# Kept rows turned by VectorE in 32x32 blocks and stored features outermost, in place of transposes on TensorE

## The reference

```python
def _L0_attn_ref(x, w_gate, w_up, w_down):
    s = jax.nn.silu(jnp.einsum('bsh,ih->bsi', x, w_gate))     # I = 2752 features
    k = int(0.5 * I)
    _, idx = jax.lax.top_k(-jnp.abs(s), k)                    # the half smallest in magnitude, per token
    flat = flat.at[rows, idx.reshape(B * S, k)].set(0.0)      # ... become zero
    s = s * jnp.einsum('bsh,ih->bsi', x, w_up)
    return jnp.einsum('bsi,hi->bsh', s, w_down)
```

## Time and profile before

| | |
|---|---|
| median of 3 runs | 1417.43 us (1416.8 to 1418.82) |
| span of the profiled execution | 1417.5 us |
| TensorE matmuls busy | 1372.4 us, 97% |
| VectorE busy | 967.6 us, 68% |
| GpSimd busy | 941.6 us, 66% |
| ScalarE busy | 738.9 us, 52% |
| DMA packets | 111,458, of which 8,320 under 512 bytes |

### The profile page before, as it was taken

One profiled execution on the slowest core, in us unless ns is written; L12 is line 12 of the kernel. 1 busy time (PEld: TensorE's weight loads), 2 busy tenths in 40 slices (PEclk: granted clock), 3 DMA queues, 4 the chain that ended last, 5 costly groups with the idle time before them and its releaser, 6 DMA issues.

```text
span 1417.5 us, 30575 instructions
## 1 busy us (share of the span) xinstructions
PE 1372.4 (97%) x12775; PEld 1014.2 (72%) x12775; DVE 967.6 (68%) x1316; ACT 738.9 (52%) x929; POOL 941.6 (66%) x615
## 2 busy tenths in 40 slices
PE   4999999999999999899999999999999999999996
PEld 3555555555555555599999998888886788887874
DVE  6888888888888888860002998989793223255654
ACT  6788888888888888633225525151511111111211
POOL 0799888888888888714434342423333899999891
PEclk9899999999999999999999999999999999999998
DMA  9032323333323320024348357573737876865451
GB/s 355 31 104 103 135 96 115 104 117 102 125 98 107 109 95 17 26 90 155 120 141 318 120 206 226 172 253 122 256 117 239 276 250 205 268 190 183 154 200 47
DMA packets 111458, 217.92 MB, mean 154 GB/s; under 512 B 8320, under 2 KB 84176, under 8 KB 106320
## 3 DMA queue, kind: packets, MB, share of 16 engines
q1 hardware_dynamic: 90128, 192.93, 39.6%
q10 hardware_dynamic: 21184, 22.96, 5.3%
HBM read 173.66 MB, written 42.21 MB: 152 GB/s over the span
## 4 chain that ended last, share of the span: by engine, by line
PE 90%; DVE 3%; ACT 2%; DMA 1%; issue 1%; POOL 1%; SPq 0%; DVEq 0%; ACTq 0%; POOLq 0%
PE fast_psum L1979 17%; PE fast_psum L1871 16%; PE fast_psum L2009 15%; PE fast_psum L1889 15%; PE fast_psum L1956 14%; PE fast_psum L1908 6%; PE fast_psum L1915 1%; PE fast_psum L2039 1%; PE fast_psum L1993 1%; PE fast_psum L2060 1%; DMA fast_d_raw<-w_down 1%; PE fast_psum L1894 1%; ACT fast_below L1722 1%; PE fast_psum L1838 1%; ACT fast_g_hi L1694 1%
## 5 line engine op out<-in xcount | busy, mean ns | idle before, releaser
L1308 DVE TENSOR_TENSOR fast_masked<-fast_psum,fast_mask_t 128x1024 f32<-128x1024 f32 (+1 forms) x416 | 488.0, 1218 | 72.6 <-PE fast_psum L1871 70.9
L1164 POOL TENSOR_TENSOR fast_pair<-fast_probs 128x1024 f32<-128x1024 f32 x192 | 457.2, 2384 | 96.7 <-PE fast_psum L1908 47.8
L1639 ACT ACTIVATE fast_probs<-fast_masked 128x1024 f32<-128x1024 f32 (+1 forms) x416 | 437.7, 1057 | 68.9 <-DVE fast_masked L1308 53.9
L1871 PE MATMUL fast_psum<-fast_qT,fast_kraw 32*128 32x256 f32 (+1 forms) x3328 | 247.0, 403 | 6.8 <-ACT fast_qT L1586 3.2
L1889 PE MATMUL fast_psum<-fast_probs,fast_vraw 128*32 128x256 f32 (+1 forms) x3328 | 226.5, 386 | 0.8 <-ACT fast_probs L1639 0.8
L1871 PEld LDWEIGHTS fast_psum<-fast_qT,fast_kraw 32*128 32x128 f32 (+1 forms) x3328 | 153.7, 182 | 93.3 <-DVE fast_masked L1308 53.9
L1219 POOL TENSOR_TENSOR fast_d_lo<-fast_d_raw,fast_d_hi 128x256 fp32r<-128x256 f32 (+1 forms) x264 | 198.8, 783 | 5.3
L1195 POOL TENSOR_TENSOR fast_g_lo<-fast_g_raw,fast_g_hi 128x2752 fp32r<-128x2752 f32 x14 | 86.1, 6150 | 143.0 <-ACT fast_g_hi L1694 121.0
L1956 PE MATMUL fast_psum<-fast_g_hi,fast_z_hi 128*128 128x344 f32 x512 | 164.8, 322 | 2.0 <-POOL fast_g_lo L1195 2.0
L1889 PEld LDWEIGHTS fast_psum<-fast_probs,fast_vraw 128*32 128x32 f32 (+1 forms) x3328 | 87.1, 109 | 107.3 <-ACT fast_probs L1639 46.5
L1956 PE MATMUL fast_psum<-fast_g_lo,fast_z_hi 128*128 128x344 f32 x512 | 163.6, 320 | 0.0
(11 more groups left out here) (161 smaller groups left out, 1889.7 us busy)
## 6 DMA issues: line engine op xcount, KB each, us to landing
fast_d_raw<-w_down SPq DMA_DIRECT2D x63, 512.0 KB, 3.8
fast_kraw<-ctx_t SPq DMA_DIRECT2D x32, 800.5 KB, 5.9
fast_vraw<-ctx_nat SPq DMA_DIRECT2D x16, 1536.0 KB
fast_g_raw<-w_gate SPq DMA_DIRECT2D x15, 1376.0 KB, 7.2
s<-fast_res SPq DMA_DIRECT2D x16, 688.0 KB, 3.8
fast_mag<-s SPq DMA_DIRECT2D x8, 1376.0 KB, 9.3
fast_sx<-s SPq DMA_DIRECT2D x8, 1376.0 KB, 6.7
sk<-fast_sx SPq DMA_DIRECT2D x8, 1376.0 KB, 7.0
```

The source lines that it names most:

```text
L1164: pool.tensor_tensor(pair[:, n % PAIR_BUFS], both[:, :, 0, :], both[:, :, 1, :], ALU.add).then_inc(paired, 1)
L1308: dve.tensor_tensor(into, of, m, ALU.add).then_inc(mask_added, 1)
L1639: act.activation(probs[0:r, g % RING, hp * HALF:(hp + 1) * HALF], masked[0:r, h % SLOTS, :], ACT.Exp).then_inc(exp_done, 1)
L1871: last = pe.matmul(scores[0:r, (2 * g + hp) % SLOTS, h % 2, i * 256:(i + 1) * 256], kraw[b % BUFS][q, u, c * P:c * P + r], qT[q, b, u, :], ...
```

## The change

VectorE gets one more instruction per tile. `keep` writes its result over `near` and not over `sx`, and `turn_kept` transposes `near` into `sx` in 32x32 blocks. A store in four parts, one for each 32 partitions, then puts these blocks in memory with the features outermost, as `s_t`; the pieces are 32 values long. The down stage loads `t_s`, a block's kept rows with features on partitions, and VectorE multiplies it with `t_u` without a transpose on TensorE. `sx` has two buffers, and the last tile uses a buffer of `mag`. The orders of SP and ScalarE change with it.

```diff
-        sx = at("sx", WIDE + 4 * I, [I])[:, :]
+        sx_of = [at(f"sx{j}", start, [I])[:, :] for j, start in enumerate((WIDE + 4 * I, THIN + 2 * HT * NJ))]
+        sx = [sx_of[t % 2] for t in range(TILES - 1)] + [mag[(TILES - 3) % MAGS]]
+        t_s = [at(f"t_s{j}", T_S + TW * j, [TW]) for j in range(TURNS)]
...
-        UP_SK_AT = {1: 1, 5: 2, 7: 3, 12: 4, 13: 5, 18: 6, 20: 7}
+        UP_STORE_AT = {1: 1, 5: 2, 7: 3, 12: 4, 14: 5, 19: 6}
+        UP_SX_AT = {0: 2, 2: 3, 6: 4, 8: 5, 13: 6, 15: 7}
...
             def load_sx(t):
-                if t >= 1:
-                    sp.wait_ge(sk_stored, 16 * t)
-                sp.dma_start(sx, s[t * P:(t + 1) * P, :]).then_inc(sx_full, 16)
-
-            def store_sk(t):
-                sp.wait_ge(kept, t + 1)
-                sp.dma_start(sk[t * P:(t + 1) * P, :], sx).then_inc(sk_stored, 16)
+                if t == 1:
+                    sp.wait_ge(g_lo_done, LOADS)
+                elif t == TILES - 1:
+                    sp.wait_ge(kept, t - 1)
+                elif t >= 2:
+                    sp.wait_ge(st_stored[t % 2], 16 * QUARTERS * (t // 2))
+                sp.dma_start(sx[t], s[t * P:(t + 1) * P, :]).then_inc(sx_full, 16)
+
+            def store_turned(t):
+                sp.wait_ge(sx_turned, t + 1)
+                if t == TILES - 1:
+                    sp.wait_ge(st_stored[t % 2], 16 * QUARTERS * (t // 2))
+                for q in range(QUARTERS):
+                    sp.dma_start(s_t.rearrange("(b r) n -> r b n", r=BLK)[:, :, t * P + q * BLK:t * P + (q + 1) * BLK],
+                                 sx[t][q * BLK:(q + 1) * BLK, :].rearrange("r (b n) -> r b n", n=BLK)
+                                 ).then_inc(st_stored[t % 2], 16)
...
                 if p + 1 == PASSES:
-                    store_sk(0)
+                    load_sx(1)
+                    store_turned(0)
                     load_mag(3)
-                    load_sx(1)
...
-                if f in UP_SK_AT:
-                    store_sk(UP_SK_AT[f])
-                    if UP_SK_AT[f] + 1 < TILES:
-                        load_sx(UP_SK_AT[f] + 1)
+                if f in UP_SX_AT:
+                    load_sx(UP_SX_AT[f])
+                if f in UP_STORE_AT:
+                    store_turned(UP_STORE_AT[f])
...
             load_down(2)
+            store_turned(TILES - 1)
             for n in range(STEPS):
...
-                dve.scalar_tensor_tensor(sx, near, thr[:, :], sx, ALU.is_ge, ALU.mult).then_inc(kept, 1)
+                dve.scalar_tensor_tensor(near, near, thr[:, :], sx[t], ALU.is_ge, ALU.mult).then_inc(kept, 1)
+
+            def turn_kept(t):
+                dve.wait_ge(kept, t + 1)
+                dve.transpose(sx[t], near).then_inc(sx_turned, 1)
...
-                dve.wait_ge(t_turned, n + 1)
+                dve.wait_ge(ts_full[n % TURNS], 16 * (n // TURNS + 1))
...
-                dve.tensor_tensor(t_h[n % 2][0:r, 0:w], bank[6 + n % 2][0:r, 0:w], t_u[n % TURNS][0:r, 0:w],
+                dve.tensor_tensor(t_h[n % 2][0:r, 0:w], t_s[n % TURNS][0:r, 0:w], t_u[n % TURNS][0:r, 0:w],
                                   ALU.mult).then_inc(h_ready, 1)
...
-            def load_u(n):
+            def load_factors(n):
                 gi, k = divmod(n, IC)
                 if n >= TURNS:
                     act.wait_ge(h_ready, n - TURNS + 1)
+                if k == 0:
+                    turned = max(GROUPS[gi][-1] + 1, TILES - 2)
+                    for j in range(2):
+                        act.wait_ge(st_stored[j], 16 * QUARTERS * ((turned + 1 - j) // 2))
+                m, t0 = len(GROUPS[gi]), GROUPS[gi][0]
+                act.dma_start(t_s[n % TURNS][0:rows(k), 0:m * P], s_t[k * P:k * P + rows(k), t0 * P:(t0 + m) * P]
+                              ).then_inc(ts_full[n % TURNS], 16)
...
             for n in range(STEPS):
-                if n + 2 < STEPS:
-                    turn(n + 2)
                 if n in TURN3_FIRST:
```

More of the change, by code:

```diff
@@ L627, in _, with fast @@
                 unit(B - 1, u, True)
-def fast(nc, x, ctx_nat, ctx_t, mask, x1, w_gate, w_up_t, w_down, s, sk, u_t, router_wt, router_b, a_t, b_t, all_bad, out, out_stored):
+def fast(nc, x, ctx_nat, ctx_t, mask, x1, w_gate, w_up_t, w_down, s, s_t, u_t, router_wt, router_b, a_t, b_t, all_bad, out, out_stored):
     with ExitStack() as ctx:
@@ L813, in fast @@
         sx_full = sem("sx_full")
-        sk_stored = sem("sk_stored")
-        sk_full = [sem(f"sk_full{j}") for j in range(BLOCKS)]
+        sx_turned = sem("sx_turned")
+        st_stored = [sem(f"st_stored{j}") for j in range(2)]
+        ts_full = [sem(f"ts_full{j}") for j in range(TURNS)]
         tu_full = [sem(f"tu_full{j}") for j in range(TURNS)]
-        t_turned = sem("t_turned")
         h_ready = sem("h_ready")
@@ L1766, in _ @@
                 if i == 2 * IC - 4:
-                    for q in range(2):
-                        load_block(q)
                     for n in range(TURNS):
-                        load_u(n)
+                        load_factors(n)
             def take_high(n):
@@ L1801, in _ @@
                 if n + TURNS < STEPS:
[L1802 to L1804 removed]
+                    load_factors(n + TURNS)
                 if n in ZT_AT:
@@ L1984, in _ @@
                 up(i)
-            def turn(n):
-                gi, k = divmod(n, IC)
-                q, c = n // 2, n % 2 * P
-                pe.wait_ge(sk_full[q % BLOCKS], 16 * (q // BLOCKS + 1))
-                if n >= 2:
-                    pe.wait_ge(h_ready, n - 1)
-                for i in range(len(GROUPS[gi])):
-                    last = pe.transpose(bank[6 + n % 2][0:rows(k), i * P:(i + 1) * P],
-                                        t_sk[q % BLOCKS][:, i, c:c + rows(k)], eye[:, :])
-                last.then_inc(t_turned, 1)
             def down(n, i):
```

37 lines of the change are left out of this document (9 added, 28 removed).

## The result

The changed kernel takes 1444.29 us (median of 4 runs, 1443.08 to 1445.88), the kernel before 1418.12 us (4 runs, 1416.8 to 1419.26): a ratio of 1.0181, interval 1.0165 to 1.0197. It is slower by 26 us, where 14 us were forecast.

What follows compares the result with a forecast made beforehand. TensorE was taken as the bound, GpSimd 0.23 us per step behind it in down. Transposes and multiply together +2, store pieces +12.3, turn 0: 1417.5 + 14 = 1431.5, given as 1431 us, range 1412 to 1480.

Steps and rivals of the forecast that it cites:

- Part 1: Down stage: transposes leave TensorE, 19.3 us off its path; GpSimd becomes the bound, so at most -14 us.
- Part 2: Down stage: multiply t_h, now reading SBUF twice, costs GpSimd 0.35 us per step, about 0.2 in the last group.
- Part 3, the price of the pieces: Turned tile's store in 128-byte pieces: 18 ns a piece, 12.3 us of all engines per tile, against 3.7 before.
- Rival B: Small writes cost about double, 24.6 us per tile, at least +25 in up: 1469 us, up to 1495; chance 0.23.
- rival E: Stores near 54 us per tile, seven taking 378 us beside the up stage's 247: above 1550 us; chance 0.05.
- Part 3, the start of down: Start of down: last tile's store on SP's queue ahead of load_down(4) makes step 4 start 12.3 us later: +12.3.
- No later slack takes it back: Down stage from step 4: with GpSimd the bound, the 12.3 us delay at its start stays to the end.
- Part 3 and 4, the up stage: Up stage: stores of 12 to 13 us per tile just hidden under TensorE, VectorE's turns hidden too: 0.
- Part 4: VectorE: eight turns of 3.03 us, 24 us more, search ending near 1085 to 1095 us: 0, at worst +5.
- rival A: The forecast: GpSimd bounds down at about 4.58 us, last store delays step 4: 1425 to 1440 us; chance 0.50.
- the forecast's own signs: Profile after: GpSimd medians rise, steps 4.5 to 4.6 us, small packets +88,064, step 4 cast near 1125, up DMA share 0.83.
- two signs against it: The forecast is wrong if down steps fall to 4.2 us, or TensorE waits for w_up in the up stage.

Runs made afterwards that it cites:

- experiment 1: Changed kernel with one operand of the multiply t_h read from a PSUM bank in place of t_s: 1431.6 us, ratio to before 1.0096.
- Experiment 2: Changed kernel with the last tile's store issued in step 8 of the down stage and not before it: 1439.48 us.
- Experiments 4: Changed kernel with VectorE's turn cut to one block of 32 columns, all stores and waits kept: 1439.22 us.
- 11: Changed kernel, w_down cast on ScalarE in steps 0 to 33, SyncE stores one transfer at a time, tiles 6 and 7 stored in down, tile 7 turned there: 1428.95 us.
- 12: Kernel of 11 with ScalarE's sums and comparisons for the third and fourth pair of tiles two or three copies later: 1418.1 us, ratio to before 1.0009.

## Why the prediction was right or wrong

- **Part 1** (at most -14 us from the transposes): right. With the contention gone, experiment 1, the way from step 4 to the last addition is 10.7 us shorter than before, where 13.8 were worked out (260.9 against 274.7). The first two thirds are as forecast, 169.9 us for 169.2; the last one takes 94.8 and not 91.7.
- **Part 2** (the multiply costs GpSimd 0.35 us a step): right in kind, shown by experiment 1, too large in size: 0.20 us. GpSimd's step is 4.41 us and not 4.58. The net of both parts was put at +2 us and is +2.5; the last third takes 99.3 us (before 96.6), and not 94, which made up for the smaller step. That the net came out so near is luck: two errors of 5 us cancel. With the PSUM operand both durations fall at once. The Trainium skill's "SBUF — State Buffer", "Who interferes with whom", says that an instruction of VectorE with two SBUF inputs contends with GpSimd's reads and one with a single SBUF input doesn't; the trace agrees, with 865 and 557 ns.
- **Part 3, the price of the pieces**: 12.3 us of engine time a tile was forecast, some 9.3 measured (13.5 ns a piece and not 18). Rival B's 24.6 us a tile is not what these pieces show, rival E's 54 still less. The Trainium skill's rule that transfers below 512 bytes are done by read-modify-write ("DMA: Bandwidth & Descriptors", "Specifications") names no price; no run here shows a price doubled over the 12.3 us.
- **Part 3, the start of down**: +12.3 forecast, +10.1 measured, by the step named (the last store in SyncE's queue ahead of the loads of w_down). Experiment 2 gives 11.5 from the end of up to step 4. The size rests on other terms than the sum's: not 12.3 us of engines but 13.2 us of standing queue, less the 5.8 us by which the next load lands faster. "No later slack takes it back" was right: the changed kernel is 20.7 us behind at step 4 and 20.5 at the end of the second third.
- **Part 3 and 4, the up stage**: this term failed. It was put at 0, as "just hidden", and is +10.6 us. Part 3 compared two times, the landing of w_up near 933 us and the need for it at 933, and took the tie as no cost, though it noted that each us beyond it would come back in several stores. Two terms were too small. The store of tile 2 was put at 914, two turns later than before (907.9 + 6.1); but it also waits for its own turn, so three turns make 917, and it left at 918.4. And the load of w_up was given 3.4 us from its issue to its landing, where the earlier trace rows has 5.0. That the load still left at 930.1, where the sum had put it (926 + 3.6), is chance: SyncE was done with the store at 926.3, but the engines were busy with it until 930 (share 0.90 from 919 to 930 us). From there mag's 3.6 us and the 5.0 of the load give 938.6, and GpSimd got the block at 938.8. TensorE stood 4.8 us; the lower clock behind the stop cost another 2.3. All waits together are 7.4 us, so some 0.9 of the 10.6 us are not assigned. The prediction asked for the DMA share of the stage (0.83 forecast, 0.70 measured), a mean that says nothing of the 20 us in which it was 0.98.
- **Part 4** (3.03 us a turn): exact, 3.05. But its slack was misread. The search ended at 1075 us before, so 24 us more nearly fit before the first multiply at 1095, and it ended at 1098.9 in the trace, before up did. What was overlooked is that VectorE's results are waited for inside the stage: the store waits for the turn, ScalarE's comparison for the cut, and both stand in queues of which TensorE's weights are the next item. Experiments 4 (6.0 us), 11 and 12 (5.5 us) show it.

So the time came out at 1444 us where 1431 were forecast: of the 13 us between them 10.6 are the up stage and 3.9 the part by which the medians differ more than the spans; the start of down gives 2.2 back. 1444 lies above the 1425 to 1440 of rival A, whose mechanism was right in down. It lies inside 1412 to 1480 only because that range reached up for rival B's dearer pieces, which aren't what filled it.

Of the forecast's own signs these held: small packets +88,976, GpSimd waits little for TensorE (6.4 us), TensorE waits for d_lo (14.2 us), t_h up to 1.39 us with a median of 0.89. These did not: steps are 4.41 us and not 4.5 to 4.6, step 4's cast starts at 1133.08 and not near 1125, and the medians of GpSimd's subtractions (741 and 742 ns) and casts (1040 and 1039) did not rise; only the mean of the subtractions of 128x256 did, from 783 to 847 ns, so the median was the wrong thing to ask for. Of the two signs against it one came true: TensorE waited for u_lo, so for w_up, in the up stage.

## What to carry to other kernels

A slack is not the distance to the end of a stage: ask for each later result of an engine who waits for it first, and what stands behind that waiter in its queue. Count a delay's own step too: the store of tile 2 waits for three turns, not for two. Where two times in a sum meet within a few us, count the tie as a cost: here the lower clock behind a stop added half of it again. Work taken from the bounding engine is worth only the distance to the next one, here 0.23 us a step, and the operand that replaces it must not slow that one.
